# Reading f32 weights directly in four stages of an eight-core layer, and rewriting two feed-forward mirrors in the weights' own layout during the transformer heads

## The reference

```python
xn = _layernorm(x, axis=-1)
s = _L0_attn_ref(xn, ...)          # retention
g = _silu(_L0_ffn_ref(xn, ...))    # routed transformer layer
x = x + s * g

# retention: q, k, v = split(x @ w_qkv); xpos on q and k;
#   y = ((q k^T) * D**-0.5 * decay mask) v;  yn = group norm of y per head
#   return (silu(x @ w_g) * yn) @ w_proj
# routed layer, by argmax(x @ w_router.T):
#   0: x + simple_bias
#   1: x + x @ w_down.T @ w_up.T
#   2: xn1 = layer_norm(x); causal softmax attention with wq, wk, wv;
#      x2 = x + ctx @ wo.T;  x2 + gelu(layer_norm(x2) @ w_ff1.T) @ w_ff2.T
```

## Time and profile before

| | us |
|---|---|
| median of two timed runs | 6535.07 (6525.72 to 6544.43) |
| profiled execution, device time | 6497.98 |
| profiled execution, span of the slowest core | 6496.4 |
| spans of the eight cores | 6430.4 to 6496.4 |
| TensorE busy | 3832.5 (59%) |
| VectorE busy | 1629.0 (25%) |
| ScalarE busy | 902.3 (14%) |
| GpSimd busy (DMA issues not counted) | 415.3 (6%) |

### The profile page before, as it was taken

The page is one execution under the profiler, slowest core; times in us unless marked ns, Lnnn a source line. Parts: engine busy times, 40 slices in busy tenths (PEclk is TensorE's granted clock), DMA queues, the critical chain, the costliest instruction groups (busy, mean ns, idle before and its releaser), DMA issues.

```text
span 6496.4 us, 63779 instructions; the slowest of 8 cores (6430.4 to 6496.4 us)
## 1 busy us (share of the span) xinstructions
PE 3832.5 (59%) x18468; PEld 1776.7 (27%) x18468; DVE 1629.0 (25%) x3980; ACT 902.3 (14%) x1869; POOL 415.3 (6%) x490
## 2 busy tenths in 40 slices
PE   1376676676664222117455656556565557997877
PEld 1223333333332000002123323233232223443333
DVE  6613323233332000005622122222222122001222
ACT  2101111111111000001022121221212101110000
POOL 0001111111110111110000000000000000000000
PEclk9987787777876666558666767668677788998888
DMA  3137776655564778992100000000000112335454
GB/s 106 52 45 82 80 78 67 72 57 66 66 65 51 74 70 82 92 88 65 43 12 17 18 12 23 12 15 21 12 23 6 60 60 88 115 114 177 177 174 150
DMA packets 659450, 436.67 MB, mean 67 GB/s; under 512 B 573856, under 2 KB 598688, under 8 KB 649920
## 3 DMA queue, kind: packets, MB, share of 16 engines
q0 software_dynamic: 599616, 319.06, 33.1%
q1 hardware_dynamic: 59520, 113.54, 5.2%
HBM read 558.65 MB, written 159.38 MB: 111 GB/s over the span
## 4 chain that ended last, share of the span: by engine, by line
PE 51%; DMA 16%; DVE 16%; issue 10%; ACT 5%; DVEq 1%; ACTq 0%; SPq 0%; POOLq 0%; POOL 0%
DMA ff1T_bf<-ff1T 7%; DMA ff2T_bf<-ff2T 6%; PE pbA L871 5%; PE pbB L871 4%; PE pbA L1841 3%; PE pbB L812 3%; PE pbB L1841 3%; PE pbA L812 3%; PE pbA L1701 3%; PE pbB L1701 3%; PE pbA L753 2%; ACT scp L1042 2%; PE pbA L1017 2%; PE pbY L1119 2%; PE pbS L1119 2%
## 5 line engine op out<-in xcount | busy, mean ns | idle before, releaser
L1284 PE MATMUL pbA<-xn_ownT,wqh 128*128 128x512 bf16 x256 | 90.5, 531 | 658.3 <-DMA wqh<-wg_bf 658.3
L871 PE MATMUL pbA<-xn_allT,wvh 128*128 128x512 bf16 x1024 | 296.6, 455 | 38.0 <-DVE vtok L897 13.7
L1119 PE MATMUL pbY<-vtok,scT_sb 128*128 128x128 bf16 x1024 | 126.6, 301 | 279.0 <-DVE scT_sb L1103 279.0
L871 PE MATMUL pbB<-xn_allT,wvh 128*128 128x512 bf16 x1024 | 258.4, 411 | 52.5 <-DVE vtok L897 40.2
L1701 PE MATMUL pbA<-bufA,wqh 128*128 128x512 bf16 x1024 | 234.2, 382 | 70.7 <-DVE bufA L1664 68.1
L1841 PE MATMUL pbA<-xn_allT,wff 128*128 128x512 bf16 x1024 | 227.3, 383 | 76.8 <-DMA xn_allT<-hg_sp 76.8
L1088 PE MATMUL pbT<-eye_sb,scp 128*128 128x128 bf16 x2304 | 267.8, 291 | 0.7
L1119 PE MATMUL pbS<-vtok,scT_sb 128*128 128x128 bf16 x1280 | 119.8, 256 | 235.2 <-DVE scT_sb L1103 235.2
L812 PE MATMUL pbA<-xn_allT,wkh 128*128 128x512 bf16 x1024 | 237.4, 386 | 1.2 <-PE pbD L783 0.3
L812 PE MATMUL pbB<-xn_allT,wkh 128*128 128x512 bf16 x1024 | 237.5, 386 | 0.2 <-DVE kb_sb L828 0.2
L897 DVE COPY vtok<-pbT 128x512 bf16<-128x512 bf16 x128 | 54.3, 424 | 726.1 <-PE pbT L889 726.1
(11 more groups left out here) (291 smaller groups left out, 5403.7 us busy)
## 6 DMA issues: line engine op xcount, KB each, us to landing
wff<-ff2T_bf POOLq DMA_DIRECT2D x32, 2048.0 KB, 8.1
ff1T_bf<-ff1T POOLq DMA_DIRECT2D x64, 512.0 KB, 8.2
ff2T_bf<-ff2T POOLq DMA_DIRECT2D x16, 2048.0 KB, 25.5
wqh<-ff1T_bf POOLq DMA_DIRECT2D x64, 512.0 KB, 4.6
wqkvTf_bf<-wqkvT_f POOLq DMA_DIRECT2D x48, 512.0 KB, 6.8
p0x<-x_all SPq DMA_DIRECT2D x16, 1024.0 KB, 6.0
xn_allT<-hg_sp SPq DMA_DIRECT2D x2, 8192.0 KB, 37.4
p0x<-x_own SPq DMA_DIRECT2D x8, 1024.0 KB, 6.0
```

The costliest lines, as they stand in the source:

```text
L871: inst = t.matmul(pb[key][:, 0:cw], self.wv_h[buf][:, ct, :], self.xn_allT[:, ct, c0:c0 + cw], start=(ct == 0), stop=(ct == CT - 1))
L1119: inst = t.matmul(pb[ykey][:, 0:P], self.scT_sb[:, st * P:(st + 1) * P], self.vtok[:, st * P:(st + 1) * P], start=(st == 0), stop=(st == n ...
L1284: inst = t.matmul(pb[key][:, 0:cw], self.wq_h[buf][:, ct, :], self.xn_ownT[:, ct, c0:c0 + cw], start=(ct == 0), stop=(ct == CT - 1))
```

## The change

The mirrors of `w_g`, `w_proj`, `woT` and `wqkvT_f` are removed with their conversions. The gate stage, the projection, the output projection and the transformer heads load their tiles from the f32 weights, converting on the way, as the retention heads do. The two mirrors that stay, `ff1T_bf` and `ff2T_bf`, take the shape of their weights, (2048, 8192) and (8192, 2048), so a conversion copies whole rows, and a load takes a slice of 128 columns, 256 bytes of each row. Each is converted in 8 steps of one DMA (2M elements, 8 MB read, 4 MB written), ff1T first, in one stream. The sixteen steps are issued one in each transformer head, and none in retention heads, gate and projection turns; the drain of what is left moves behind the transformer heads.

```diff
--- before.py
+++ after.py
@@ -185,12 +185,8 @@
         x2_sp = dint("x2_sp", [C, OWN])
         hg_sp = dint("hg_sp", [F, OWN])
 
-        wg_bf = dint("wg_bf", [C, C])
-        wproj_bf = dint("wproj_bf", [C, C])
-        wqkvTf_bf = dint("wqkvTf_bf", [3 * C, C])
-        woT_bf = dint("woT_bf", [C, C])
-        ff1T_bf = dint("ff1T_bf", [F, C])
-        ff2T_bf = dint("ff2T_bf", [C, F])
+        ff1T_bf = dint("ff1T_bf", [C, F])
+        ff2T_bf = dint("ff2T_bf", [F, C])
 
         r3 = lambda ap: ap.rearrange("(a p) n -> p a n", p=P)
         self.wqkv_r = r3(w_qkv)
@@ -200,14 +196,8 @@
         self.woT_r = r3(woT)
         self.ff1T_r = r3(ff1T)
         self.ff2T_r = r3(ff2T)
-        mirv = lambda m: m.rearrange("(k p) (c j) -> k p c j", p=P, j=P)
-        castv = lambda w: w.rearrange("(c p) (k j) -> k p c j", p=P, j=P)
-        self.wgbf_s = mirv(wg_bf)
-        self.wprojbf_s = mirv(wproj_bf)
-        self.wqkvTfbf_s = mirv(wqkvTf_bf)
-        self.woTbf_s = mirv(woT_bf)
-        self.ff1Tbf_s = mirv(ff1T_bf)
-        self.ff2Tbf_s = mirv(ff2T_bf)
+        self.ff1Tbf_r = r3(ff1T_bf)
+        self.ff2Tbf_r = r3(ff2T_bf)
         wdT_r = r3(w_downT)
         wrT_r = r3(wrT)
         xall_r = x_all.rearrange("(tt p) c -> tt p c", p=P)
@@ -293,30 +283,25 @@
             self.pc = {}
             self.pump = []
 
-            def _mkcast(stream, dst4, src4, k0, k1, key):
+            def _mkcast(stream, dst, srcw, r0, r1, key):
                 def go():
                     def _(g):
-                        for k in range(k0, k1):
-                            self.dma(g, stream, dst4[k], src4[k])
+                        self.dma(g, stream, dst[r0:r1, :], srcw[r0:r1, :])
                     self.G(_)
                     if key is not None:
                         self.pc[key] = self.tok(self.dsem(stream))
                 return go
 
-            def _fill(stream, mir4, srcv, key, nch):
-                K = mir4.shape[0]
+            def _fill(stream, mir, srcw, key, nch):
+                K = mir.shape[0]
                 nch = min(nch, K)
                 bounds = [K * i // nch for i in range(nch + 1)]
                 for i in range(nch):
-                    self.pump.append(_mkcast(stream, mir4, srcv,
+                    self.pump.append(_mkcast(stream, mir, srcw,
                                              bounds[i], bounds[i + 1],
                                              key if i == nch - 1 else None))
-            _fill("pc0", self.wgbf_s, castv(w_g), "wg", 2)
-            _fill("pc0", self.wprojbf_s, castv(w_proj), "wproj", 2)
-            _fill("pc0", self.woTbf_s, castv(woT), "wo", 2)
-            _fill("pc1", self.wqkvTfbf_s, castv(wqkvT_f), "qkvTf", 8)
-            _fill("pc1", self.ff1Tbf_s, castv(ff1T), "ff1", 10)
-            _fill("pc1", self.ff2Tbf_s, castv(ff2T), "ff2", 6)
+            _fill("pc1", ff1T_bf, ff1T, "ff1", 8)
+            _fill("pc1", ff2T_bf, ff2T, "ff2", 8)
 
             def _(v):
                 self.wt(v, consts_sq, consts_sp)
@@ -562,7 +547,6 @@
                                    apply_ready=late_ready, rowp=64)
             self.emit_gate_proj(cvv, fill_gate=sa0 + sa1 + so,
                                 fill_proj=ta0 + ta1)
-            self.pump_drain()
             self.dbg_dump("s", None, [C, OWN], [], dram=s_sp, guards_dma=list(self.proj_sqd))
             ln1a_tok = self._ln_tok
             late_ready.append(self.proj_tok)
@@ -574,6 +558,7 @@
 
             self.emit_attention("ffn", bufA, ctx_sp=self.ctx_sp_r,
                                 ready=[ln1a_tok, ln1o_tok])
+            self.pump_drain()
             self.dbg_dump("ctx", None, [C, OWN], [], dram=ctx_sp,
                           guards_dma=[self.attn_done[3]])
 
@@ -684,32 +669,18 @@
         cfg = self.cfg
         buf = h % 2
         C = cfg.C
-        H = cfg.H
-        if kind == "ret":
-            wsrc = self.wqkv_r
-
-            def _(g, h=h, buf=buf):
-                self.wt(g, *self.g_w[buf], *self.g_w2[buf], *self.mem_guard)
-                self.dma(g, f"wh{buf}", self.wq_h[buf].ap(),
-                         wsrc[:, :, 0 * C + h * P:0 * C + (h + 1) * P])
-                self.dma(g, f"wh{buf}", self.wk_h[buf].ap(),
-                         wsrc[:, :, 1 * C + h * P:1 * C + (h + 1) * P])
-                self.dma(g, f"wh{buf}", self.wv_h[buf].ap(),
-                         wsrc[:, :, 2 * C + h * P:2 * C + (h + 1) * P])
-            self.G(_)
-            wtok = self.tok(self.dsem(f"wh{buf}"))
-        else:
-            def _(g, h=h, buf=buf):
-                self.wt(g, *self.g_w[buf], *self.g_w2[buf], *self.mem_guard,
-                        self.pc["qkvTf"])
-                self.dma(g, f"wh{buf}", self.wq_h[buf].ap(),
-                         self.wqkvTfbf_s[0 * H + h])
-                self.dma(g, f"wh{buf}", self.wk_h[buf].ap(),
-                         self.wqkvTfbf_s[1 * H + h])
-                self.dma(g, f"wh{buf}", self.wv_h[buf].ap(),
-                         self.wqkvTfbf_s[2 * H + h])
-            self.G(_)
-            wtok = self.tok(self.dsem(f"wh{buf}"))
+        wsrc = self.wqkv_r if kind == "ret" else self.wqkvTf_r
+
+        def _(g, h=h, buf=buf):
+            self.wt(g, *self.g_w[buf], *self.g_w2[buf], *self.mem_guard)
+            self.dma(g, f"wh{buf}", self.wq_h[buf].ap(),
+                     wsrc[:, :, 0 * C + h * P:0 * C + (h + 1) * P])
+            self.dma(g, f"wh{buf}", self.wk_h[buf].ap(),
+                     wsrc[:, :, 1 * C + h * P:1 * C + (h + 1) * P])
+            self.dma(g, f"wh{buf}", self.wv_h[buf].ap(),
+                     wsrc[:, :, 2 * C + h * P:2 * C + (h + 1) * P])
+        self.G(_)
+        wtok = self.tok(self.dsem(f"wh{buf}"))
         ttok = None
         if kind == "ret":
             def _(g, h=h, buf=buf):
@@ -741,7 +712,7 @@
             buf = h % 2
             if h + 1 < H:
                 self.load_head(h + 1, kind)
-            if kind == "ret":
+            if kind == "ffn":
                 self.pump_step()
 
             for ci, (c0, cw) in enumerate(cfg.own_chunks):
@@ -1261,12 +1232,11 @@
             buf = dct % 2
 
             def _(g, dct=dct, buf=buf):
-                self.wt(g, *self.g_w[buf], *self.mem_guard, self.pc["wg"])
+                self.wt(g, *self.g_w[buf], *self.mem_guard)
                 self.dma(g, f"wh{buf}", self.wq_h[buf].ap(),
-                         self.wgbf_s[dct])
+                         self.wg_r[:, :, dct * P:(dct + 1) * P])
             self.G(_)
             wload[dct] = self.tok(self.dsem(f"wh{buf}"))
-            self.pump_step()
             yld_box = []
 
             def _(s, dct=dct, buf=buf):
@@ -1324,12 +1294,11 @@
             buf = ct2 % 2
 
             def _(g, ct2=ct2, buf=buf):
-                self.wt(g, *self.g_w2[buf], self.pc["wproj"])
+                self.wt(g, *self.g_w2[buf])
                 self.dma(g, f"wk{buf}", self.wk_h[buf].ap(),
-                         self.wprojbf_s[ct2])
+                         self.wproj_r[:, :, ct2 * P:(ct2 + 1) * P])
             self.G(_)
             wl = self.tok(self.dsem(f"wk{buf}"))
-            self.pump_step()
             for ci, (c0, cw) in enumerate(cfg.own_chunks):
                 key = "A" if ci % 2 == 0 else "B"
 
@@ -1538,9 +1507,9 @@
             buf = ct2 % 2
 
             def _(g, ct2=ct2, buf=buf):
-                self.wt(g, *self.g_w[buf], self.pc["wo"])
+                self.wt(g, *self.g_w[buf])
                 self.dma(g, f"wh{buf}", self.wq_h[buf].ap(),
-                         self.woTbf_s[ct2])
+                         self.woT_r[:, :, ct2 * P:(ct2 + 1) * P])
             self.G(_)
             wl = self.tok(self.dsem(f"wh{buf}"))
             for ci, (c0, cw) in enumerate(cfg.own_chunks):
@@ -1689,7 +1658,7 @@
             def _(g, ft=ft, buf=buf):
                 self.wt(g, *self.g_w[buf], self.pc["ff1"])
                 self.dma(g, f"wh{buf}", self.wq_h[buf].ap(),
-                         self.ff1Tbf_s[ft])
+                         self.ff1Tbf_r[:, :, ft * P:(ft + 1) * P])
             self.G(_)
             wl = self.tok(self.dsem(f"wh{buf}"))
             for ci, (c0, cw) in enumerate(cfg.own_chunks):
@@ -1817,7 +1786,7 @@
                 def _(g, ct2=ct2, buf=buf):
                     self.wt(g, *g_wff2[buf], *self.mem_guard, self.pc["ff2"])
                     wl_q.append(self.dma(g, f"wf2{buf}", wff2[buf][:, :, :],
-                                         self.ff2Tbf_s[ct2]))
+                                         self.ff2Tbf_r[:, :, ct2 * P:(ct2 + 1) * P]))
                 self.G(_)
 
                 sl_box = []
```

## The result

The changed kernel takes 0.9106 of the time of before, 95% interval 0.9048 to 0.9163; its profiled execution took 5953.8 us, against 6498.0. The forecast was 5960 us, 8.8% less than before; 8.9% less was measured. So stages are compared on cores without that: core 2 of the changed kernel first of all.

What follows compares the result with a forecast made beforehand. Gate-stage weight loads queued behind GpSimd's conversions were taken to hold up TensorE. 6498 - 684 + 4 + 3 + 104 = 5925, plus 37 between profiled and timed runs, rounded 5960 us; range 5855 to 6200 us.

Steps and rivals of the forecast that it cites:

- Part 1: Gate stage: without conversions in its loop, sixteen turns of 13.9 us plus extras give 236 us against 920, gain 684 us.
- Parts 2 and 3: Retention heads lose 108 conversions, gain 0; projection pays +4 us for direct w_proj loads, output projection 0 for woT.
- Part 4: Transformer heads: three f32 loads and one conversion take at most 72 us of a 117 us head, so cost 0.
- 24 and 51 us of its bounds: Transformer heads: price of one 2M-element conversion, 24 us from a long-run row, 51 us from a doubled short-run row.
- Rival 3: Transformer heads: long conversions do not spread over 16 engines; on one engine 378 us each, about 10,140 us total; chance 0.04.
- Part 5: Feed-forward A and B: 256-byte runs of the new mirrors make loads slower, +3 us in A and +104 us in B.
- 32 ns a run: Feed-forward loads: engine time of a 256-byte run, on a line between 26.6 ns (128 bytes read) and 42.9 ns (512).
- the 16.4 ns of the earlier trace: Feed-forward loads: lowest price of a run, from a light hardware-queue load with 256-byte rows; B loads 8.4 us, hidden.
- 25 to 38 ns: Feed-forward loads: price of a run under which the forecast itself holds, 5900 to 6060 us; chance 0.45.
- rival 1: Feed-forward A and B: short runs are cheap (16.4 ns), loads stay behind matmuls, B +7, total 5862 us; chance 0.22.
- slower matmuls behind a gap: Feed-forward B: a 3 us gap may slow TensorE's next group by 2 us, within time already awaiting DMA.
- The 37 us: Whole kernel: the median of timed runs, 6535, lies 37 us above the profiled execution, so 5925 + 37 was forecast.

Runs made afterwards that it cites:

- e2: Kernel before, with only the ff1T and ff2T conversions moved to the transformer heads, all six mirrors and tile layout kept: 0.8877 of before, profiled 5809.4 us.
- e3: Changed kernel with its sixteen conversion steps issued one in each gate turn, none in transformer heads: gate stage 663 us, core 7 ends at 6269.6 us.
- e4: Changed kernel without any mirror, feed-forward A and B loading straight from f32 weights, converting on the way: 0.9624 of before; A 530, B 991 us.
- e5: Changed kernel with the 32 wff loads issued by SyncE on the hardware queue instead of GpSimd: B 646 us, all cores at 5787 to 5823 us.
- e7: Changed kernel with each wff load cut in two DMAs of 4096 runs on two streams: 0.9033 of before, B 668 us.
- e1: Changed kernel with ff1T_bf and ff2T_bf kept in the layout by tiles, converted in transformer heads: A 446, B 642 us; cores 0 to 3 at 5781 to 5802 us.
- e6: Changed kernel with 256 bytes more between the rows of both mirrors: 0.9043 of before; B 696 us, A 453 us.

## Why the prediction was right, and where it was off

By its own parts, with core 2 of the changed kernel against core 7 of before (the table of stages):

| part | forecast us | measured us |
|---|---|---|
| 1 gate stage | -684 | -672 |
| 2 retention heads | 0 | not told from its spread |
| 3 projection, output projection | +4 | +2 and 0 |
| 4 transformer heads | 0 | -2 |
| 5 feed-forward A | +3 | +9 |
| 5 feed-forward B | +104 | +54 |

**Part 1 held**, and e2 and e3 show the mechanism: with everything as before but the place of two conversions the stage takes 250 us, and with the steps back in it 663. What was missed, 12 us, is mostly the start: TensorE waits 10.0 us for the first `wqh<-w_g`, two such loads being issued at once. Before the change, the list of conversions set the end of the stage: cores 2 and 7 spent 1596 and 1622 us in the retention heads and reached the projection at the same time, 2965.2 and 2964.9. So on core 7, with the longest heads, the stage's gain is among the smaller ones.

**Parts 2 and 3 held** within what can be told. The output projection hid its f32 loads.

**Part 4 held.** A conversion landed 34.9 us (ff1T) and 40.1 us (ff2T) after its issue on core 2, between the 24 and 51 us of its bounds, so the three loads and a conversion take about half a head. Rival 3, a block that does not spread over the engines, is refuted by that: one engine would have taken 378 us.

```profile
wff<-ff2T_bf POOLq DMA_DIRECT2D x32, 2048.0 KB, 15.3
ff1T_bf<-ff1T POOLq DMA_DIRECT2D x8, 4096.0 KB, 34.9
ff2T_bf<-ff2T POOLq DMA_DIRECT2D x8, 4096.0 KB, 40.1
...
wqh<-ff1T_bf POOLq DMA_DIRECT2D x64, 512.0 KB, 5.9
```

**Part 5 named the right loads and summed them wrongly.** Three steps failed: the price of 32 ns a run, taken on the line between two converting loads; no term in stage B for a load's time beyond its packets; and the assumption that the packets of one load follow those of the last, so that the engines' time is the turn. In A the load landed 5.9 us after its issue, as forecast (5.8), and TensorE waited for it 6.3 us in 11 waits (1.4 in 3 before). In B, one `wff` load of the changed kernel, core 2, issued at 5298.90:

```profile
5298.90 2.76 POOL L133 DMA_DIRECT2D wff<-ff2T_bf  x1 [12.54 <-DVE cb_t L1837]
```

```profile
q0 software_dynamic: 528, 2.10, 55.2%
```

2.10 MB went in 528 packets, not 8192: sixteen runs of 256 bytes in each. 0.552 x 16 x 17.1 / 528 = 286 ns a packet, 17.9 ns a run. That is nearly the 16.4 ns of the earlier trace rows, a plain copy, which I had as the lower bound, and outside the 25 to 38 ns of the forecast. The earlier trace rows are converting copies, which move one run a packet, and e4 shows that price (47 ns) where runs are converted. So the row nearest in kind was the plain one, not the ones nearest in number and queue. That its number fits so well is chance: it is single runs on the hardware queue, which took 26 ns each in e5. The Trainium skill has a figure that bears on this: its page DMA: Bandwidth & Descriptors, SWDGE vs HWDGE vs iDMA, says that a packet preferably holds up to 4096 bytes and at most 64 descriptors. This trace agrees for plain software loads, 16 x 256 bytes a packet, and does not for converting ones, one run a packet.

By its price a run is rival 1's, but its loads are not hidden as rival 1 had it (+54 us where it had +7), because of the other two steps. Beyond its packets (33 an engine x 286 ns = 9.4 us) the load needs 5.9 us to land. The first 2.75 us of that is GpSimd writing descriptors, the row above. So the load is not bound by its bytes, as I had it (17.1 us a turn), but lands 15.3 us after an issue that waits for the turn two before. Turns of the first half, and TensorE's kinds of wait for a DMA in stage B, core 2:

```profile
5233.17 16.92 PE L1810 MATMUL pbA<-xn_allT,wff 128*128 128x512 bf16 x64 [51.96 <-DMA xn_allT<-hg_sp]
...
5250.34 13.99 PE L1810 MATMUL pbB<-xn_allT,wff 128*128 128x512 bf16 x64
...
5266.69 15.54 PE L1810 MATMUL pbA<-xn_allT,wff 128*128 128x512 bf16 x64 [2.04 <-DMA wff<-ff2T_bf]
...
5282.47 13.99 PE L1810 MATMUL pbB<-xn_allT,wff 128*128 128x512 bf16 x64
...
5298.73 13.97 PE L1810 MATMUL pbA<-xn_allT,wff 128*128 128x512 bf16 x64 [1.96 <-DMA wff<-ff2T_bf]
...
5473.42 13.97 PE L1810 MATMUL pbB<-xn_allT,wff 128*128 128x512 bf16 x64 [1.44 <-DMA wff<-ff2T_bf]
```

```profile
PE pbA L1810 <- DMA xn_allT<-hg_sp: 82.5, 2, 52.0
...
PE pbA L1810 <- DMA wff<-ff2T_bf: 27.9, 14, 3.1
...
PE pbB L1810 <- DMA wff<-ff2T_bf: 12.7, 10, 1.5
```

From the third turn to the sixteenth a turn takes (5473.42 - 5266.69)/13 = 15.9 us, 1.7 more than before. 28 such turns are 48 us, and the two transfers of `hg_sp` are awaited 6 us longer (82.5 against 76.8 us on core 7 of before): that accounts for the 54 us. In TensorE's rows the same time stands as 27.9 + 12.7 = 40.6 us in 24 waits for `wff`, the 6 us, and 10 us more of busy time (485.8 instead of 475.7). The prediction had named slower matmuls behind a gap (2 us) and costed them at nothing. Four of the 24 late turns have them, 15.54 to 15.66 us; the other 20 take 13.97. Which gap has this effect is not shown.

Two things set the 15.9 us. The first is the double buffer: the turn's matmuls (14.4 us), 1.1 us until the issue and 15.2 us until the landing are 30.7 us for two turns, 15.4 a turn. The second is in no wait of the program: GpSimd did not issue a load of 8192 runs while another one was under way, though that writes another buffer and has another stream. The first two loads of stage B need nothing of each other. They were issued, before the change (core 7), after it (core 2), and in e7, where a load is two halves (core 2), at:

```profile
5859.41 0.55 POOL L133 DMA_DIRECT2D wff<-ff2T_bf  x1 [0.30 <-issue]
5860.21 0.53 POOL L133 DMA_DIRECT2D wff<-ff2T_bf  x1 [0.24 <-issue]
```

```profile
5183.89 2.78 POOL L133 DMA_DIRECT2D wff<-ff2T_bf  x1 [0.28 <-issue]
5205.05 2.76 POOL L133 DMA_DIRECT2D wff<-ff2T_bf  x1 [18.38 <-issue]
```

```profile
5167.50 5.07 POOL L133 DMA_DIRECT2D wff<-ff2T_bf  x3 [0.27 <-issue]
5180.18 1.69 POOL L133 DMA_DIRECT2D wff<-ff2T_bf  x1 [7.61 <-issue]
```

Two loads of long runs go 0.8 us apart. Of the loads of 8192 runs the first landed 20.8 us after its issue, and only then was the second issued. In e7 three halves go at once and the fourth when the first has landed, 12.3 us after its issue. So 12,288 runs were under way together and 16,384 never. It is the same in the turns. In the changed kernel 23 of 30 loads are issued later than 1.1 us after the matmuls that free their buffer, by 18 us in all; in e4 29 of 30, 5.6 to 14.5 us after them; in e7 28 of 30 pairs at 1.1 us. How much of the 54 us this holding back makes, beside the double buffer, no run tells.

What the runs do show of the 54 us: with the tiles' layout all of it is gone (e1); on the hardware queue, where GpSimd writes no descriptors, the turns are 14.23 us (e5); with half loads 28 us are gone (e7); 256 bytes of padding do nothing (e6). The price of a run was little more than half of what I had put, the time beyond the packets was left out, and the stage's cost was half.

The forecast landed within 0.2% of the profiled execution, and that is partly chance. Part 5 was charged about 45 us too much. The slowest core of the profiled execution spent 1670 us in the retention heads, with its lower granted clock, where core 2 spent 1612; that is about as much in the other direction. The 37 us that the sum adds for the difference of executions cover part of it. Against cores 2 and 3, 5875 and 5881 us, the forecast is 1.4% high.

What stays open: why a load that is issued by GpSimd takes some 3 us beyond its packets and the writing of its descriptors; and why short runs move at half the rate of long ones, 17.9 ns for 256 bytes against 9.6 (4.9 us an engine for 512 runs' bytes). e6 excludes only 256 bytes of padding as a cure. It is also open what keeps a second load of 8192 runs from being issued.

## What to carry to other kernels

A transfer's place in its issuer's program order can cost more than its bytes: the 68 conversions issued in the gate stage cost some 670 us only because weight loads of 512 KB stood behind them, and nothing when the same queue carried them through a stage with slack. When a layout is simplified along the way, price it apart from the move: here the move alone (e2) was worth 11%, and the simpler layout took 66 us of that back. For the price of a transfer, take the row of the same kind (plain or converting) before the row of the same size, and keep its packets' time and the time beyond them apart. Where a load has many short runs, look in the trace whether the next one is issued before it lands: here two buffers did not put two such loads under way.

## What the hardware showed beyond that

- The software queue moves a converting copy one run a packet (2064 packets for 2048 runs; 47 ns a run in e4) and a plain copy sixteen runs of 256 bytes a packet (528 packets for 8192 runs, 17.9 ns a run).
- The hardware queue sends the same 8192 runs as single packets, at 26 ns of an engine each against 17.9, and still lands them 1.8 us earlier (13.5 against 15.3 us).
- Software loads of 4096 runs were under way three at a time (e7), those of 8192 runs one at a time (changed kernel and e4), those of 128 long rows two at a time (before).
- A load of 8192 runs keeps GpSimd 2.75 us in writing descriptors, one of 4096 runs 1.68 us, one of 2048 runs 1.15 us, one conversion of 2M elements in long runs 0.54 us.
- Under conversions that hold the DMA engines at 0.40 in the transformer heads, TensorE's, VectorE's and ScalarE's work there took as long as under 0.05: 1875 against 1877 us.
